# GpSimd adds the fourth pair of channel tiles into y for every second state

## The reference

```
def step(h, xs):
    d_t, B_t, C_t, u_t = xs
    dA = jnp.exp(d_t[..., None] * A)
    h = h * dA + (d_t * u_t)[..., None] * B_t[:, None, :]
    y_t = jnp.einsum('bdn,bn->bd', h, C_t)
    return (h, y_t)
...
y = jnp.moveaxis(ys, 0, 1) + u * D_param
y = y * jax.nn.silu(gate)
```

## Time and profile before

| | us |
|---|---|
| median of 3 runs | 3846.74 (3846.54 to 3847.21) |
| the profiled execution | 3846.44 |
| its span, first to last instruction | 3844.6 |
| DVE busy | 3323.2 (86%) |
| PE busy | 3318.4 (86%) |
| ACT busy | 2488.6 (65%) |
| POOL busy | 2469.7 (64%) |

### The profile page before, as it was taken

The page is one execution under the profiler, slowest core; times in us unless marked ns, Lnnn a source line. Parts: engine busy times, 40 slices in busy tenths (PEclk is TensorE's granted clock), DMA queues, the critical chain, the costliest instruction groups (busy, mean ns, idle before and its releaser), DMA issues.

```text
span 3844.6 us, 46273 instructions
## 1 busy us (share of the span) xinstructions
PE 3318.4 (86%) x12672; PEld 2368.1 (62%) x12672; DVE 3323.2 (86%) x6128; ACT 2488.6 (65%) x4790; POOL 2469.7 (64%) x1943
## 2 busy tenths in 40 slices
PE   4878785799999999999999999999999999985738
PEld 4656563576666666667676767676766666663525
DVE  5889885189898989999999989898989898989891
ACT  5666663176767676767676867676867676755550
POOL 0444444068677776868696959595959596957470
PEclk9889897899999999999999999999999999987868
DMA  2212211201111111111111111111111111111010
GB/s 99 77 60 76 67 58 43 106 23 44 26 47 27 46 28 45 36 45 31 42 31 42 39 34 41 34 39 34 42 34 39 37 39 36 39 34 36 20 36 6
DMA packets 119377, 165.36 MB, mean 43 GB/s; under 512 B 8544, under 2 KB 84192, under 8 KB 118624
## 3 DMA queue, kind: packets, MB, share of 16 engines
q1 hardware_dynamic: 119136, 162.63, 15.1%
HBM read 128.39 MB, written 25.69 MB: 40 GB/s over the span
## 4 chain that ended last, share of the span: by engine, by line
POOL 26%; DVE 19%; PE 18%; issue 15%; ACT 3%; DVEq 1%; POOLq 0%; DMA 0%; SPq 0%; ACTq 0%
POOL dBu L850 15%; DVE D L1292 11%; POOL yacc L863 11%; PE W L1048 6%; PE W L1098 5%; DVE prod L1311 2%; PE W L1121 2%; DVE D L1314 2%; PE W L1125 2%; PE D L1048 1%; DVE yacc L1323 1%; DVE U L1243 1%; PE W L1080 1%; ACT L900 1%; DVEq L1290 1%
## 5 line engine op out<-in xcount | busy, mean ns | idle before, releaser
L1292 DVE TENSOR_TENSOR_SCAN D<-D,hc,dBu 128x256 f32<-128x256 f32 x2048 | 1434.8, 738 | 47.0 <-ACT D L991 47.0
L850 POOL TENSOR_TENSOR dBu<-U,BC 128x512 f32<-128x512 f32 x1024 | 1295.9, 1277 | 274.9 <-DMA BC<-bc_scratch 190.7
L1048 PE MATMUL W<-nT,wffn 128*128 128x256 f32 x5632 | 1241.5, 382 | 47.0 <-ACT nT L889 32.6
L1048 PEld LDWEIGHTS W<-nT,wffn 128*128 128x128 f32 x5632 | 1059.0, 189 | 230.0 <-ACT nT L889 37.7
L991 ACT ACTIVATE D<-delta,A 128x256 f32<-128x256 f32 x2048 | 891.6, 468 | 425.5 <-DVE yacc L1323 404.5
L863 POOL TENSOR_TENSOR yacc<-yacc,prod 128x512 f32<-128x512 f32 x736 | 934.3, 1269 | 262.4 <-DVE prod L1311 258.0
L1080 PE MATMUL W<-wffn,hT 128*128 128x512 f32 (+1 forms) x1408 | 640.6, 612 | 42.4 <-DVE hT L1205 42.4
L1080 PEld LDWEIGHTS W<-wffn,hT 128*128 128x128 f32 (+1 forms) x1408 | 273.0, 197 | 373.8 <-issue 323.0
L1311 DVE TENSOR_TENSOR prod<-D,BC 128x512 f32<-128x512 f32 x736 | 492.8, 670 | 0.0
L1048 PE MATMUL W<-nT,win 128*128 128x256 f32 x2048 | 454.1, 383 | 33.6 <-ACT nT L889 33.6
L1048 PEld LDWEIGHTS W<-nT,win 128*128 128x128 f32 x2048 | 391.5, 192 | 106.4 <-ACT nT L889 44.8
(11 more groups left out here) (117 smaller groups left out, 3270.6 us busy)
## 6 DMA issues: line engine op xcount, KB each, us to landing
BC<-bc_scratch SPq DMA_DIRECT2D x256, 256.0 KB, 4.6
XM<-x_scratch SPq DMA_DIRECT2D x29, 512.0 KB, 5.2
X<-x_scratch SPq DMA_DIRECT2D x17, 512.0 KB, 3.6
ix<-idx SPq DMA_DIRECT2D x33, 255.0 KB, 2.8
X<-x SPq DMA_DIRECT2D x16, 512.0 KB, 3.9
XR<-x SPq DMA_DIRECT2D x16, 512.0 KB, 3.7
x_scratch<-XR SPq DMA_DIRECT2D x16, 512.0 KB, 3.0
out<-X SPq DMA_DIRECT2D x16, 512.0 KB, 2.8
```

The costliest lines, as they stand in the source:

```text
L850: nc.gpsimd.tensor_tensor(dBu[e % 4][:], U[:, 2 * j:2 * j + 2, :], BC[slot][:, 0:1, :].to_broadcast([P, 2, CH]), ALU.mult).then_inc(s_dBu, 1)
L1048: last = T_.matmul(dst, lhsT, rhs, start=(n == 0), stop=(n == len(terms) - 1))
L1292: V.tensor_tensor_scan(D[:, m, :], D[:, m, :], dBu[e % 4][:, m % 2, :], hc[:, n, m:m + 1], ALU.mult, ALU.add).then_inc(s_scan, 1)
```

## The change

In the first 14 chunks the fourth pair (j = 3) is treated like the other three when n is odd. For these 8 elements of a chunk DVE writes the product into prod, POOL adds it to yacc, and ACT saves the last column. For even n the fourth pair stays as it was. POOL has then 56 sums in such a chunk instead of 48, DVE 8 instead of 16. The last two chunks are unchanged. The counts of the semaphores are worked out by a new function `sums`, and the sum that stays on DVE now also waits for POOL's sums up to pair e-4.

```diff
-        def pool_pairs(f1):
-            return 3 if f1 else 2
...
+        def by_pool(f1, e):
+
+            n, j = divmod(e, 4)
+            return j < 3 or n % 2 == 1 if f1 else j < 2
+
+        def sums(f1, e):
+
+            return sum(by_pool(f1, k) for k in range(e))
 
         def pool_sums(i):
 
-            return S * (3 * i - steps_less(i))
+            return sum(sums(k < NC - 2, NE) for k in range(i))
 
         def dve_sums(i):
 
-            return S * (i + steps_less(i))
+            return NE * i - pool_sums(i)
...
                     def add(e):
 
                         n, j = divmod(e, 4)
-                        r = pool_pairs(f1) * n + j
+                        r = sums(f1, e)
                         pool.wait_ge(s_prod, NE * i + e + 1)
                         if r == 0:
                             pool.wait_ge(m_skip, ME * (i + 1))
                         if n:
-                            pool.wait_ge(s_acc, pool_sums(i) + r - pool_pairs(f1) + 1)
+                            pool.wait_ge(s_prod, NE * i + e - 3)
+                            pool.wait_ge(s_acc, pool_sums(i) + sums(f1, e - 3))
                         y = yacc[:, 2 * j:2 * j + 2, :]
                         nc.gpsimd.tensor_tensor(y, y, prod[r % 2][:], ALU.add).then_inc(s_acc, 1)
...
                     for e in range(NE):
                         if e + 4 < NE:
                             outer(e + 4)
-                        if e % 4 < pool_pairs(f1):
+                        if by_pool(f1, e):
                             add(e)
...
-                        if j < pool_pairs(f1):
+                        if by_pool(f1, e):
                             act.wait_ge(s_prod, NE * i + e + 1)
                             N_.activation(hc[:, n, 2 * j:2 * j + 2], D[:, 2 * j:2 * j + 2, CH - 1], ACT.Copy).then_inc(s_ha, 1)
...
                     def times_c(e):
 
                         n, j = divmod(e, 4)
-                        h_, r = D[:, 2 * j:2 * j + 2, :], pool_pairs(f1) * n + j
+                        h_, r = D[:, 2 * j:2 * j + 2, :], sums(f1, e)
...
-                        if j < pool_pairs(f1):
+                        if by_pool(f1, e):
                             dve.wait_ge(s_acc, pool_sums(i) + max(r - 1, 0))
                             dve.wait_ge(s_scan, 2 * NE * i + 2 * e + 2)
                             V.tensor_tensor(prod[r % 2][:], h_, c_, ALU.mult).then_inc(s_prod, 1)
...
                     def add(e):
 
                         n, j = divmod(e, 4)
-                        pair, mine = slice(2 * j, 2 * j + 2), 4 - pool_pairs(f1)
+                        pair = slice(2 * j, 2 * j + 2)
                         dve.wait_ge(m_skip, ME * (i + 1))
+                        dve.wait_ge(s_acc, pool_sums(i) + sums(f1, e - 3))
                         dve.wait_ge(s_prod, NE * i + e - 3)
...
-                        if 2 <= e <= NE + 1 and (e - 2) % 4 >= pool_pairs(f1):
+                        if 2 <= e <= NE + 1 and not by_pool(f1, e - 2):
                             add(e - 2)
```

More of the change, by code:

```diff
@@ L730, in side_late @@
             return 1 - SIDE_EARLY if f1 else SIDE_EARLY
-        def pool_pairs(f1):
-            return 3 if f1 else 2
-        def steps_less(i):
-            return max(i - (NC - 2), 0) if isinstance(i, int) else 0
+        def by_pool(f1, e):
[3 more added lines that the diff above has]
+            return sum(by_pool(f1, k) for k in range(e))
         def pool_sums(i):
-            return S * (3 * i - steps_less(i))
+            return sum(sums(k < NC - 2, NE) for k in range(i))
         def dve_sums(i):
-            return S * (i + steps_less(i))
+            return NE * i - pool_sums(i)
         def rows(p):
@@ L986, in step @@
                             save(e - 4)
-                            act.wait_ge(s_ha, pool_sums(i) + pool_pairs(f1) * (n - 1) + min(j + 1, pool_pairs(f1)))
+                            act.wait_ge(s_ha, pool_sums(i) + sums(f1, e - 3))
                         else:
@@ L1297, in save @@
                         n, j = divmod(e, 4)
-                        if j >= pool_pairs(f1):
+                        if not by_pool(f1, e):
                             dve.wait_ge(s_scan, 2 * NE * i + 2 * e + 2)
@@ L1312, in times_c @@
                         else:
-                            dve.wait_ge(s_hd, dve_sums(i) + (4 - pool_pairs(f1)) * n + j - pool_pairs(f1) + 1)
+                            dve.wait_ge(s_hd, dve_sums(i) + e + 1 - sums(f1, e))
                             V.tensor_tensor(h_, h_, c_, ALU.mult).then_inc(s_hC, 1)
@@ L1318, in add @@
                         n, j = divmod(e, 4)
-                        pair, mine = slice(2 * j, 2 * j + 2), 4 - pool_pairs(f1)
+                        pair = slice(2 * j, 2 * j + 2)
                         dve.wait_ge(m_skip, ME * (i + 1))
+                        dve.wait_ge(s_acc, pool_sums(i) + sums(f1, e - 3))
                         dve.wait_ge(s_prod, NE * i + e - 3)
-                        dve.wait_ge(s_hC, dve_sums(i) + mine * n + j - pool_pairs(f1) + 1)
+                        dve.wait_ge(s_hC, dve_sums(i) + e + 1 - sums(f1, e))
                         V.tensor_tensor(yacc[:, pair, :], D[:, pair, :], yacc[:, pair, :], ALU.add).then_inc(s_prod, 1)
```

## The result

The changed kernel takes **3920.45 us** (median of 4 runs, 3920.43 to 3920.84), the kernel before 3846.97 us on the same chip: a ratio of 1.0191 (1.0175 to 1.0207). It is slower by 73.5 us, 5.25 us for each of the 14 changed chunks, where 0.63 us was forecast, and it lies far above the range. The profiled execution took 3920.84 us, with a span of 3919.0.

A forecast was written before the change was run, and what follows sets the result against it. DVE was taken as the bound, with POOL nearly full and becoming slower. Per chunk -0.2 + 0.6 - 0.65 + 0.88 = +0.63 us, over 14 chunks +8.8, gave 3855.5 us; range 3834 to 3870.

The forecast's parts named there:

- the price of the shared port: DVE and POOL sharing a read port was to cost only part of the +0.6 us at the statistics behind step 49.
- the step on nmr: Behind step 52, nmr waits 0.4 us for rstd, then lasts until POOL's instruction ends: 1.05 us, against 0.16 with POOL idle.
- the terms without the port: Per chunk: -0.2 us left at pair 48, 0.4 nmr's wait for rstd, -0.65 from state 13, +0.88 at the chunk's end.
- the rule: Every added POOL sum blocks DVE up to 1.23 us through the shared port: 138 us more, 3993 us; chance below 0.01.
- the worst case: Bound per chunk: 0.2 and 0.65 us lost too, signals 0.1 more at ten or so held products: +2.3 us, +32 in all.
- POOL without a gap from sum 8 to sum 48: Ten states, 75 POOL operations of 1.226 us back to back, 91.95 us; 0.2 us of DVE's gain left at pair 48.
- The held products: DVE's products wait for POOL's sums, a few tenths of a us each, in odd states and the even ones after.
- The chunk's end: From product 62 to the gate 3.33 us instead of 2.45, +0.88 us, with DVE idle for about 2 us.
- The forecast sign of nmr waiting for rstd behind step 52: The trace should show nmr behind step 52 preceded by a wait for POOL's rstd.
- The wait for rstd: At the statistics behind step 49, DVE's nmr was to wait 0.4 us for POOL's rstd.
- rival (b), an even trade: The body of a chunk gains 0.8 us and the tail takes it, 3847 us; chance one in four.
- (d): Held products make DVE late for gated products and PE stalls: +1.5 to +2.3 us a chunk, 3867 to 3878; chance 0.11.

The follow-up runs named there:

- run 5: Changed kernel with veps and nmr kept on DVE, each as two one-column instructions, rstd as pointer scalar: 3845.36 us, ratio 0.9992.
- run 6: Kernel before the change with veps and nmr on DVE in the same one-column form: 3820.67 us, ratio 0.9929.
- runs 2 and 3: veps moved from DVE to POOL and nmr to ACT, in the changed kernel (3845.08 us) and in the kernel before (3822.64 us).
- run 11: Changed kernel with nmr alone in one-column form, veps as it was: 3871.04 us, ratio 1.0058.
- run 10: Changed kernel with veps on POOL and nmr on ACT, and the last state's fourth sum back on DVE (55 POOL sums a chunk): 3826.07 us, ratio 0.9945.
- run 1: Changed kernel with the nmr of step 26 put behind step 4: 3895.93 us, ratio 1.0124.
- run 13: Changed kernel with the nmr of step 26 put behind step 16: 3920.77 us, one execution.
- run 14: Changed kernel with the nmr of step 26 put behind step 20: 3929.50 us, one execution.
- run 12: Changed kernel with veps alone in one-column form, nmr as it was: 3919.28 us, ratio 1.0184.
- run 4: Kernel before the change with 24 extra small POOL instructions a chunk, in the first 14 chunks, whose result nobody reads: 3871.65 us, ratio 1.0062.
- run 8: Changed kernel with the nmr of step 26 put behind step 12: 3892.09 us, one execution.

## Why the prediction was wrong

**The step that failed** is the price of the shared port: "By the rows the shared port costs a part of the 0.6 us above." It rests on the step on nmr, "It then lasts until POOL's instruction ends". The rows behind that were right (1.05 us beside a busy POOL, 0.16 beside an idle one), and for the nmr of step 52 it came true, 1.06 us. But it was priced there alone. The change takes POOL's gaps away, and I had worked that out myself: "That is robust as long as POOL has no gap in those 92 us". In those 92 us stands the nmr of step 26, and just behind them the veps of step 50; both were put at nothing, without a reason, as if they stayed at 0.45 and 1.08 us. They measured 5.45 and 3.73.

What this cost: with both in the form that the port doesn't catch (runs 5 and 6) the change costs 24.7 us and not 73.5. So 48.8 us, 3.5 of the 5.25 us a chunk, are the longer nmr and veps, and runs 2 and 3 give 3.6 by another way. Freeing nmr alone gives the same 3.5 (run 11). The other 1.76 us a chunk, where the terms without the port made +0.43, was mis-sized; see below. I had bounded the port's cost by the rows of the kernel before, all of them taken with a POOL that had gaps. That bound holds nothing for the changed kernel.

The weighing of the Trainium skill's "Perfetto Trace Analysis", section "Optimizing Scalar/DVE Operations", fell on the wrong side for the same reason. Its warning about the shared port came true, not through scans and products, which kept 739 and 674 ns, but through two small instructions a chunk, 28 in all. I gave the rule less than 0.01 since I tried it on all operations or on none. The 3993 us that I worked out for it was wrong in the other direction.

A slip in the bounds: the worst case as I described it, 0.2 and 0.65 us lost and 1.0 for ten signals, adds up to +2.5 us a chunk and not +2.3. The measured +5.25 lies outside either.

**What held.** POOL without a gap from sum 8 to sum 48: in run 5, where no port stall breaks it, POOL's sums follow one another without idle time between these two, the last gap before and the first behind:

```profile
1384.03 1.27 POOL L866 TENSOR_TENSOR yacc<-yacc,prod 128x512 f32<-128x512 f32 x1 [0.97 <-DVE prod L1316]
...
1493.15 1.27 POOL L866 TENSOR_TENSOR yacc<-yacc,prod 128x512 f32<-128x512 f32 x1 [0.47 <-DVE prod L1316]
```

The held products are as expected, 0.21 us in the row shown (44.9 us in all there). The chunk's end:

```profile
1536.23 1.26 DVE L1314 TENSOR_TENSOR prod<-D,BC 128x512 f32<-128x512 f32 x2
1539.50 2.36 DVE L1224 TENSOR_TENSOR sgm<-yacc,sgm 128x1024 f32<-128x1024 f32 x2 [2.01 <-POOL yacc L866]
...
1536.97 2.49 POOL L866 TENSOR_TENSOR yacc<-yacc,prod 128x512 f32<-128x512 f32 x2 [0.62 <-DVE prod L1314]
```

3.27 us from product 62 to the gate, 3.33 were forecast, and 2.01 of them idle. The counts (848 and 176) are exact, POOL's added busy time is 129.5 us for 140, and scans wait for ACT 46.9 us as before. The forecast sign of nmr waiting for rstd behind step 52 is missing in the changed kernel, where veps has just emptied POOL, and is there in run 5.

**What was mis-sized.** Without the port's stalls the change costs 24.7 us (run 5 less run 6), 1.76 us a chunk. My terms without the port make -0.2 + 0.4 - 0.65 + 0.88 = +0.43. The wait for rstd was 1.20 us and not 0.4:

```profile
1490.26 0.33 DVE L1201 TENSOR_SCALAR nmr<-mv,rstd 128x1 f32<-128x1 f32 x2 [1.20 <-POOL rstd L834]
```

That is 0.8 of the 1.3 us that are missing. Of the other 0.5, about half is the wait for PE ahead of the chunk's scans, named at run 10: 3.6 and 4.7 us by turns in run 5, 3.9 in run 6. The other half is no cost of every chunk: from the first gate to the fourteenth the two kernels part by 1.52 us a chunk ((3376.70 - 958.97 - 3353.77 + 955.79) / 13), the first chunk alone by 3.2, and the rest comes behind the fourteenth. In the time of run 5 against its own runs of the kernel before (3845.36 and 3848.01) this cost doesn't show, since the one-column form gives 27.3 us, 1.95 a chunk, back by itself (run 6). My rival (b), an even trade, so came out in run 5 for a reason that it didn't name.

**The rivals.** (d), clearly slower, had the sign; its +1.5 to +2.3 us a chunk covers the 1.76 that is left without the port's stalls, but by luck for the most part, since 0.8 of that is the wait for rstd, and PE's part in run 5 is about 0.25. Of the whole loss its 3867 to 3878 us reached less than half. My expectation for run 1 repeated the error from the other side, in taking DVE's standing still for loss: 5.0 us more in nmr cost 3.5 a chunk (run 11), since POOL still had work while nmr stood.

## What to carry to other kernels

Before work is moved to GpSimd, list the VectorE instructions that share its port (two SBUF tensor inputs, or a two-column SBUF to SBUF tensor_scalar) in the stretch where GpSimd will become gap-free, and cost each of them not at one GpSimd instruction but at up to the time until GpSimd runs out of ready work. Look for their duration in the trace, not for idle time: a port wait shows as a 128x2 instruction of 5.45 us on a busy engine. Such small instructions are best written so that they don't need the port (one column at a time, the second operand as a pointer scalar), which was worth 0.7% in the old kernel before anything was moved, and 1.1% together with a smaller move, four sums a chunk. A trace of the kernel before can't give this price, and one chunk of the kernel after isn't enough either: compare the instruction in all of them.

## What the runs showed of the hardware

**A VectorE instruction at the shared port can starve.** It isn't always released at the end of the GpSimd instruction that it met. In the changed kernel it stood through four further ones and ended 0.02 us after the last (1450.48 and 1450.46). The Trainium skill, "SBUF — State Buffer", section "SBUF: two separate sides", says that whichever starts first gets the shared pair for the whole instruction while the other blocks. The trace agrees as to who blocks. By that rule the wait would be one instruction at most, some 1.3 us in these rows, and nmr at step 26 would have grown by no more than 14 x 0.85 = 12 us, an estimate; measured are 5.45 us each, 70 us more in all. The measurement decides.

**The form decides who is caught.** The Trainium skill, "GPSIMD Engine Reference", section "1. Specifications", names VectorE instructions with two SBUF inputs or in a two-port mode. Runs 5 and 6 agree, with means of 207 and 149 ns a column for the one-column forms, against 2014 and 1303 ns for the others in the changed kernel. That the two-column veps is caught, although it has one input, fits "Advanced Engine Details and Errata", section "Mode Summary", of the Trainium skill, where source and destination in SBUF with an even count bring the two-port mode; no run took it apart further. Scans and products, with one input in PSUM, never were caught: in the changed kernel the longest scan took 0.76 us and the longest product 0.69.

**When it slips in and when it starves** isn't settled. With a gap of POOL at most 3.3 us earlier and more POOL work ready, every instruction of the two-column form ended with the POOL instruction that it met. Behind 48 us and more without a gap, veps stood until POOL had nothing left in every chunk. Between and around these the traces go both ways. nmr stood in every chunk behind 21 us (run 13), 30 us (run 14) and 44 us (the changed kernel), and behind 53 us in run 12. But behind 44.6 us it slipped in in 12 of 13 chunks of run 4, and behind 11.9 us it stood in two chunks of run 8 and slipped in in the others (once behind 18.8). So a long run of POOL goes with the stall and doesn't decide it. How many instructions POOL had ready doesn't either: in run 8 the same three stood behind it in the chunks that slipped in and in those that stood. Nor does the length of POOL's single instructions, which lies between 1.25 and 1.35 us in long runs: nmr stood beside some of 1.25 us (run 12) and slipped past some of 1.30 (run 8). The cause stays open.
